# Causal attention in three weighing pieces, and a paired power in the norms, in an eight-layer kernel on one core

## The reference

```python
def _layernorm(x, axis=-1, eps=1e-05):
    m = jnp.mean(x, axis=axis, keepdims=True)
    v = jnp.var(x, axis=axis, keepdims=True)
    return (x - m) / jnp.sqrt(v + eps)
...
q = (x @ Wq).reshape(b, t, h, d) * scale
k = (x @ Wk).reshape(b, t, h, d) * scale
v = (x @ Wv).reshape(b, t, h, d)
dot = jnp.einsum('bqhd,bkhd->bhqk', q, k)
dot = jnp.where(causal[None, None], dot, -jnp.inf)
attn = jax.nn.softmax(dot, axis=-1)
out = jnp.einsum('bhqk,bkhd->bqhd', attn, v).reshape(b, t, h * d)
return out @ Wo
```

## Time and profile before

| what | value |
|---|---|
| median of 3 runs | 4999.79 us (4998.96 to 5003.04) |
| the profiled execution, its own time | 4999.74 us |
| its span in the trace | 4998.0 us |
| instructions in the trace | 76578 |
| PE, DVE, ACT, POOL busy | 90%, 48%, 35%, 17% of the span |

### The profile page before, as it was taken

One profiled execution on the slowest core, in us unless ns is written; L12 is line 12 of the kernel. 1 busy time (PEld: TensorE's weight loads), 2 busy tenths in 40 slices (PEclk: granted clock), 3 DMA queues, 4 the chain that ended last, 5 costly groups with the idle time before them and its releaser, 6 DMA issues.

```text
span 4998.0 us, 76578 instructions
## 1 busy us (share of the span) xinstructions
PE 4497.6 (90%) x30219; PEld 2825.7 (57%) x30275; DVE 2393.4 (48%) x6906; ACT 1724.4 (35%) x3496; POOL 842.3 (17%) x1313
## 2 busy tenths in 40 slices
PE   7988989889898898988989889898898998988989
PEld 4556545565455654557545575455754557545575
DVE  3435544355443654435544355444554445544455
ACT  2333433234332343323433234333343333433334
POOL 2003110030110301113011140111401114011140
PEclk8999979999799998999989999899998998988989
DMA  2000000000000000000000000000000000000000
GB/s 67 1 1 1 1 6 1 1 1 1 6 1 1 1 1 6 1 1 1 1 6 1 1 2 1 6 1 1 2 1 6 1 1 2 1 3 1 1 1 3
DMA packets 19571, 17.25 MB, mean 3 GB/s; under 512 B 2462, under 2 KB 18799, under 8 KB 19183
## 3 DMA queue, kind: packets, MB, share of 16 engines
q1 hardware_dynamic: 19183, 11.99, 0.8%
HBM read 9.89 MB, written 2.10 MB: 2 GB/s over the span
## 4 chain that ended last, share of the span: by engine, by line
PE 79%; POOL 7%; DVE 6%; ACT 5%; issue 3%; DVEq 0%; ACTq 0%; POOLq 0%; SPq 0%
PE banks L982 7%; PE banks L986 7%; PE banks L885 7%; PE banks L972 7%; PE banks L913 6%; PE banks L830 6%; POOL work L483 4%; PE banks L924 3%; PE banks L870 3%; PE banks L1178 3%; PE banks L1165 2%; PE banks L1199 2%; PE banks L1072 2%; PE banks L1045 2%; PE banks L1021 2%
## 5 line engine op out<-in xcount | busy, mean ns | idle before, releaser
L1367 DVE CUSTOM_DVE_ANT_0 work<-banks,mask_row 128x512 f32<-128x512 f32 (+3 forms) x1024 | 452.3, 489 | 260.7 <-PE banks L885 254.5
L885 PE MATMUL banks<-work 32*128 32x128 f32 (+3 forms) x2048 | 534.0, 550 | 24.6 <-DVE work L1367 24.6
L437 POOL TENSOR_TENSOR rstd<-rstd,half 128x1 f32<-128x1 f32 x256 | 134.2, 550 | 2470.6 <-DVE moments L1295 1899.7
L913 PE MATMUL banks<-work 32*128 32x256 f32 (+3 forms) x2048 | 527.6, 522 | 11.0 <-ACT work L643 9.1
L643 ACT ACTIVATE work<-banks 128x384 f32<-128x384 f32 (+1 forms) x768 | 374.6, 529 | 461.0 <-PE banks L913 455.2
L659 ACT ACTIVATE work<-banks 128x512 f32<-128x512 f32 (+1 forms) x384 | 228.9, 596 | 698.6 <-PE banks L982 698.4
L1439 DVE TENSOR_TENSOR work<-work,banks 128x512 f32<-128x512 f32 (+1 forms) x384 | 263.6, 686 | 355.5 <-PE banks L986 355.2
L982 PE MATMUL banks<-xnT,wg 128*128 128x512 f32 (+1 forms) x768 | 423.6, 635 | 0.0
L986 PE MATMUL banks<-xnT,wu 128*128 128x512 f32 (+1 forms) x768 | 412.0, 619 | 0.0
L972 PEld LDWEIGHTS banks<-wd,work 128*128 128x128 f32 (+1 forms) x3072 | 360.6, 191 | 57.3 <-issue 57.3
L885 PEld LDWEIGHTS banks<-work 32*128 32x128 f32 x2048 | 292.3, 222 | 166.9 <-DVE work L1367 110.4
(11 more groups left out here) (255 smaller groups left out, 7252.4 us busy)
## 6 DMA issues: line engine op xcount, KB each, us to landing
x_next<-in_L_attn_a_x_dram SPq DMA_DIRECT2D x8, 256.0 KB, 2.8
out_dram<-x SPq DMA_DIRECT2D x8, 256.0 KB, 2.2
wg<-in_L_ffn_Wg_dram SPq DMA_DIRECT2D x1, 1376.0 KB
wu<-in_L_ffn_Wu_dram SPq DMA_DIRECT2D x1, 1376.0 KB
wd<-in_L_ffn_Wd_dram SPq DMA_DIRECT2D x2, 512.0 KB
wk_l<-in_L_attn_a_Wk_dram SPq DMA_DIRECT2D x1, 512.0 KB, 7.2
wv_l<-in_L_attn_a_Wv_dram SPq DMA_DIRECT2D x1, 512.0 KB, 6.7
wq_l<-in_L_attn_a_Wq_dram SPq DMA_DIRECT2D x1, 512.0 KB, 6.8
```

Source lines behind the costliest of these rows:

```text
L885: m = eng.matmul(bank(k % 3)[:, col:col + N], q4[own, G, P * t:P * t + P], k4[own, G, 0:N], start=True, stop=True)
L913: m = eng.matmul(bank(3 + c % 3)[:, col:col + N], k4[own, G, P * s:P * s + P], q4[own, G, P * s:T], start=True, stop=True)
L1367: m = eng.tensor_tensor_reduce(out=summed[:, k % 2, col:col + N], in0=bank(k % 3)[:, col:col + N], in1=mask_row[:, T - N:T], scale=1.0, sc ...
```

## The change

It edits four places. In the norms POOL takes the power of two tiles in one instruction, after the variance of tile 1 (8th step) and of tile 3 (12th step), and DVE waits for the pair. In the causal attentions POOL masks after every column job, one block for key tiles 0 and 1 and two for key tiles 2 and 3, 12 instructions per group in place of 8. PE weighs a group in three pieces: key tile 0 after column job 7 of the same group, key tile 1 after job 11, key tiles 2 and 3 after job 3 of the next group (or at the end); each piece waits only for the masks that it reads. And the projections are spread: 0 and 1, the values, row jobs 0 to 2, then projection i followed by row job i+1 for i from 2 to 7, then the loop from row job 9.

```diff
--- before.py
+++ after.py
@@ -432,26 +432,21 @@
             return 3 + i % 4
 
         def pool_norm(eng, n):
-            for t in range(NT):
-                eng.wait_ge(normed, 12 * n + (5, 8, 11, 12)[t])
-                eng.tensor_tensor(rstd[:, t:t + 1], rstd[:, t:t + 1], half[:, 0:1],
+            for t, done in ((0, 8), (2, 12)):
+                eng.wait_ge(normed, 12 * n + done)
+                eng.tensor_tensor(rstd[:, t:t + 2], rstd[:, t:t + 2], half[:, 0:1].to_broadcast([P, 2]),
                                   ALU.pow).then_inc(rstd_ok, 1)
 
         def pool_attn(eng, n):
-            def keep(c, first, stride):
-                G, hh = c // ROWS4, column_head(c)
+            for c in range(JOBS4):
+                G, hh, j = c // ROWS4, column_head(c), c % ROWS4 // G4
                 eng.wait_ge(s_exp, JOBS4 * n + c + 1)
-                v = prob4[:, G % 2, hh, first:first + P]
-                v = bass.AP(v.tensor, v.offset, [list(v.ap[0]), [stride, 2], [1, P]])
+                v = prob4[:, G % 2, hh, C_COL[j]:C_COL[j] + P]
+                if j == 2:
+                    v = bass.AP(v.tensor, v.offset, [list(v.ap[0]), [C_COL[3] - C_COL[2], 2], [1, P]])
                 eng.affine_select(out=v, in_=v, compare_op=ALU.is_ge, fill=0.0, base=0,
-                                  pattern=[[0, 2], [1, P]], channel_multiplier=-1).then_inc(s_keep, 1)
-
-            for c in range(JOBS4):
-                j = c % ROWS4 // G4
-                if j == 1:
-                    keep(c, C_COL[0], C_COL[1] - C_COL[0])
-                elif j == 2:
-                    keep(c, C_COL[2], C_COL[3] - C_COL[2])
+                                  pattern=[[0, 2], [1, P]] if j == 2 else [[1, P]],
+                                  channel_multiplier=-1).then_inc(s_keep, 1)
 
         def mask_q(eng, c, n):
 
@@ -915,43 +910,50 @@
                     col += N
                 m.then_inc(s_col, 1)
 
-            def weigh_group(G):
-                eng.wait_ge(s_exp, JOBS4 * n + ROWS4 * (G + 1))
-                eng.wait_ge(s_keep, 2 * H * n + 2 * G4 * (G + 1))
+            def weigh_group(G, keys):
+
+                last = min(keys[-1], 2)
+                eng.wait_ge(s_keep, JOBS4 * n + ROWS4 * G + G4 * (last + 1))
                 eng.wait_ge(a_v, n + 1)
-                for s in range(NT):
+                for s in keys:
                     for hh in range(G4):
                         m = eng.matmul(bank(6 + G % 2)[32 * hh:32 * hh + 32, P * s:T],
                                        val_row[:, s, BELOW * (G4 * G + hh):BELOW * (G4 * G + hh) + 32],
                                        prob4[:, G % 2, hh, C_COL[s]:C_COL[s] + T - P * s],
                                        start=(s == 0), stop=(s == NT - 1))
-                m.then_inc(s_pv, 1)
+                if keys[-1] == NT - 1:
+                    m.then_inc(s_pv, 1)
 
             eng.wait_ge(xnT_ok, 2 * n + 1)
-            for i in range(4):
-                project(i)
+            project(0)
+            project(1)
             for t in range(NT):
                 m = eng.matmul(bank(7)[:, P * t:P * t + P], xnT[:, P * t:P * t + P], w[:, 0, :],
                                start=True, stop=True)
             m.then_inc(p_v, 1)
-            for i in range(4, 2 * NG):
+            for k in range(3):
+                score_rows(k)
+            for i in range(2, 2 * NG):
                 project(i)
-                if i % 2 == 1:
-                    for k in range(2 * (i - 5), 2 * (i - 5) + 4):
-                        score_rows(k)
-            for k in range(8, JOBS4 + LEAD):
+                score_rows(i + 1)
+            for k in range(2 * NG + 1, JOBS4 + LEAD):
                 if k < JOBS4:
                     score_rows(k)
                 if k >= LEAD:
                     c = k - LEAD
+                    G, at = c // ROWS4, c % ROWS4
                     score_columns(c)
-                    if c >= ROWS4 and c % ROWS4 == 3:
-                        weigh_group(c // ROWS4 - 1)
-                    if c >= ROWS4 and c % ROWS4 == 9:
-                        group_rows(eng, n, c // ROWS4 - 1, 6 + (c // ROWS4 - 1) % 2)
+                    if at == 7:
+                        weigh_group(G, [0])
+                    if at == 11:
+                        weigh_group(G, [1])
+                    if G >= 1 and at == 3:
+                        weigh_group(G - 1, [2, 3])
+                    if G >= 1 and at == 9:
+                        group_rows(eng, n, G - 1, 6 + (G - 1) % 2)
                 if k % ROWS4 == 2 and ROWS4 <= k < JOBS4 + 3:
                     max_columns(k // ROWS4 - 1)
-            weigh_group(NG - 1)
+            weigh_group(NG - 1, [2, 3])
             group_rows(eng, n, NG - 1, 6 + (NG - 1) % 2)
             pe_out(eng, n, w[:, 1, :], None)
 
@@ -1297,7 +1299,7 @@
                         m = eng.tensor_scalar(rstd[:, t:t + 1], moments[:, t, 1:2], EPS, None, ALU.add)
                     m.then_inc(normed, 1)
                 for t in range(NT):
-                    eng.wait_ge(rstd_ok, NT * n + t + 1)
+                    eng.wait_ge(rstd_ok, 2 * n + t // 2 + 1)
                     eng.tensor_scalar(xn[:, t, :], src[:, t, :], moments[:, t, 0:1], rstd[:, t:t + 1],
                                       ALU.subtract, ALU.mult).then_inc(xn_ok, 1)
 
```

## The result

The changed kernel takes 4969.3 us (median of 4 runs, 4966.6 to 4981.9) against 5000.2 before; the ratio is 0.994, with a 95% interval of 0.9924 to 0.9957. The forecast was 4969.

The account below looks back on a forecast made before the run. PE was taken as the bound in attention, less by its work than because others wait while it weighs; POOL in the norms. Attention's 21 us and the norms' 9.5 made 30 us, 4969 us, range 4905 to 5030.

Parts of the forecast that it names:

- Norms: In the 64 norms, pairing POOL's powers gains 1.2 us a turn, 9.5 us in eight turns.
- m: Extra time of a paired power's second element on POOL, taken as 0.09 us, between 0.002 and 0.36.
- Masks: POOL's masks in causal attention: 12 per group instead of 8, 4.0 us instead of 3.3, costed at nothing.
- Head: Start of an attention stage: first maximum 3.6 us sooner, that lead eaten by job 8, +1.0 us remaining.
- Pieces: Three weighing pieces while row jobs run: DVE idle 3.6 us a group against 3.07, together -2.3 us a stage.
- The -1.1 for two groups: While row jobs run, six pieces replacing two whole weighings cost 1.1 us a stage through DVE idle.
- Tail: End of an attention stage: only 0.3 of the last weighing's columns stay behind the last mask, +2.6 us in sum.
- The sum: Attention gains 1.0-2.3+2.6=1.3 us a stage, 21 us over 16 stages; with the norms 30 us, giving 4969 us.
- Its own signs: Timeline and POOL checks; wrong if mean power exceeds 800 ns, period leaves 11 to 14 us, or half-clock stretch moves.
- hidden pieces: In attention, three banks cover a short piece: 5.0 us gained a stage, 80 us, 4910 with the norms; chance 0.12.
- Slower, refills: In attention, first and second pieces pay length and bank refill in full, 5.0 us a group, 5027 us; chance 0.20.
- Both clock rivals: Attention's half-clock stretch shortens or leaves the maxima, 4921 us (0.13); or moves onto the alternating projections, 5030 us (0.05).

Follow-up runs that it names:

- filled kernels: Kernels with 22 repeated row jobs per causal attention stage, results unused; the changed kernel so filled took 4915.3 us, the kernel before 4934.2 us.
- head_busy_both: The kernel before with only the projections spread, plus 22 unused row jobs per attention stage: 4942.6 us, ratio 0.9877 to before.
- before_busy_both: The kernel before with 22 unused row jobs added per attention stage, otherwise as it was: 4934.2 us, ratio 0.9864 to before.
- attn_busy_both: The changed kernel with single powers instead of pairs, plus 22 unused row jobs per attention stage: 4933.8 us, ratio 0.9860 to before.

## Why the prediction was right, and where it was wrong

The time was right within 1 us; of the working, the pieces' idle and the shape of the tail were right, and the sum was not.

- **Norms.** Wrong in size: m is 0.153, not 0.09, so of the 0.46 at full clock 0.15 is left, and none of it reaches the copy, behind two transposes that now follow each other. Alone the edit gave 5 us (0.9991), not 9.5; the forecast of a gain by itself has no support at full clock (2.80 against 2.79).
- **Masks.** Right: 12 in place of 8 per group (294 and 408 ns in the profile after). Every piece behind row-strip products starts as these end, so no mask held one up but the last of a stage.
- **Head.** The first shift came 0.96 us sooner in attention a, as forecast (1.0), but only 0.1 sooner in attention b, in profiles with half clock at different places. On the filled kernels, with it in like places, the new head is 0.2 us sooner in attention a (24.96 against 25.13 in turn 4 of `head_busy_both` and `before_busy_both`) and 1.0 later in attention b (25.57 against 24.56). The lead of the first maximum was there (4.0 us in a, 2.7 in b), and was more than eaten: job 8's maximum came 0.5 us later than before in a and 1.8 later in b. Alone the edit cost 21 us, which no term had.
- **Pieces.** Forecast 3.6 us of DVE idle a group, measured 3.7; the idle of 1.3, 0.9 and 1.42 was 1.40, 0.79 and 1.53. The -1.1 for two groups was put in the wrong place: the steady period did not grow, but on the filled kernels the interval before the second shift did, by 1.45, and the one before the last by 0.24. That every piece starts as the last row-strip product ends is what the Trainium skill's rule says (TensorEngine Tiling (Array Packing), Key Properties), that a change of tiling mode drains TensorE. What it costs is not one price: the wait for the weights was 0.76, 0.32 or 0.13.
- **Tail.** The last weighing went from 3.76 to 0.86, against the forecast's 0.3 of 3.76. But 1.4 of the 2.9 us were half clock; at full clock on the filled kernels, 2.36 became 0.86 and the copy behind it came 1.15 us sooner, where the term's 2.6 had 1.5 for full clock.
- **The sum.** The step that failed is "a stage gains 1.0-2.3+2.6=1.3 us, 16 stages 21 us". It took the half-clock stretches of before as fixed in place and length, and priced a change of them as two rivals of 0.13 and 0.05. At like half clock a stage does not gain 1.3 us but loses 1.4 in attention b (76.97 to 78.39). In the profile after, undisturbed stages gained 1.6 (a) and 3.0 (b), the expert layers behind them 0.9 and 0.7, a turn 6.8 us; three stages of 16 with a half-clock tail and the turns around them gave back some 24 of the 55 us. That this balance came to 31 is luck: 0.53 us of delay a turn moves it to 5013 (the median of the three shortest runs), and single powers to 5038.
- **Its own signs.** Most held: 128 powers of 703 ns, 768 masks, the three idles, the last weighing at 0.86. But the prediction called itself wrong "if the half-clock stretch moves", and it did: attention b of the third turn had 13.7 us of it from 19.9 us after its first power, and has none there in the changed kernel.

The rival "hidden pieces" fell (the idle after a piece is 0.8 to 1.5). "Slower, refills" fell by its price, 5.0 a group; what it had right is the sign at equal clock. Both clock rivals were right in part and at once: the stretch in the middle went or shortened in 14 of the 16 stages, and a new one of 13.7 us came in the tail of three.

Left open: which activity of TensorE lets the clock fall at these places. The rows show where it fell and that more row jobs there keep it up; PE's busy time as the profile counts it does not separate the cases. Why the paired powers, worth nothing by themselves, go with 69 us on the new order and 19 on the filled one is argued from the clock and not shown. Not tried: filling the other layers, and pieces for the last group alone.

## What to carry to other kernels

Where a profile shows TensorE at half clock inside a stage, a sum of removed waits is not a forecast: give the clock its own term, and compare both versions stage by stage where half clock falls in the same places; unused products in free banks make such stages common. A gain of under 1% of which the main parts lose when tried alone, or that a delay of half a microsecond turns around, points to the placement of half-clock stretches and not to a property of the order. And before rearranging a sparse stage to save waits, try filling it: 22 unused products a stage gave the old kernel 68 us and the new one 54.

## What was not expected of the hardware

- Unused work made the kernel faster by 0.8 to 1.6% in four pairs (4969.3 to 4931.9 and to 4915.3, 5002.7 to 4934.2, 5038.4 to 4956.8). The Trainium skill (TensorE: Matmul & The Clock Gate, Part 1) says that idle is the throttled state and activity releases it. The runs agree in direction: the mean clock rose from 0.912 to 0.933 with the filling of the changed kernel. That the clock also fell behind 13.60 us in which PE was busy for 12.87 is more than the sentence tells.
- Turns settle to a few lengths. In most kernels the turn that repeats took 610.9, 614.4, 617.8, 621.2, 624.6, 628.1 or 631.4 us, within some tenths and 3.4 apart: 621.2 before, 614.4 after, 624.6 with the head alone, 628.1 with the pieces alone. `attn_busy_both` alternates between 611.6 and 613.9. A small change can vanish, as the norms' did (621.2 in both), or count a whole step in nearly every turn, as the head's did.
- The clock moved layers that were not touched: the linear attention took from 103.9 to 108.5 us, with 10.2 to 23.9 us of half clock in it.
- A power on GpSimd costs 550 ns for one element a partition and 703 for two.
